# Perceiver layer on one core: the first feed-forward product by seven combined block products instead of eight plain ones, in three of its four blocks

## The reference

```
x = x + xattn(layernorm(x), ctx)
x = x + attn(layernorm(x))
x = x + ffn(layernorm(x))
ffn: h   = relu(x @ w1.T + b1)              # hidden width H = 2048
     out = q16(q8(h) @ q8(w2).T + q16(b2))  # q8: 4 exponent, 3 mantissa bits
```

## Time and profile before

| | |
|---|---|
| median of 3 runs | 946.39 us (945.07 to 947.18) |
| the profiled execution | 946.05 us, of which the span is 944.2 us |
| PE busy over the span | 926.6 us (98%) |
| DVE, ACT, POOL busy | 542.0, 583.9, 494.0 us |
| granted TensorE clock | 1.00 |

### The profile page before, as it was taken

One profiled execution on the slowest core, in us unless ns is written; L12 is line 12 of the kernel. 1 busy time (PEld: TensorE's weight loads), 2 busy tenths in 40 slices (PEclk: granted clock), 3 DMA queues, 4 the chain that ended last, 5 costly groups with the idle time before them and its releaser, 6 DMA issues.

```text
span 944.2 us, 19392 instructions
## 1 busy us (share of the span) xinstructions
PE 926.6 (98%) x7405; PEld 576.6 (61%) x7408; DVE 542.0 (57%) x980; ACT 583.9 (62%) x1095; POOL 494.0 (52%) x379
## 2 busy tenths in 40 slices
PE   6999999999999999999999999999999999999998
PEld 3556666666666666666666666666665545544443
DVE  7455655556555565555655556556677725375533
ACT  4477777777777777777777777777677122222220
POOL 2356666565566666656556666886777451110000
PEclk9999999999999999999999999999999999999999
DMA  8257576876866776677666678869875321213212
GB/s 300 68 159 141 130 131 139 163 146 130 140 135 132 137 142 128 136 155 158 132 127 145 135 135 163 185 121 182 157 141 108 90 56 40 59 33 107 88 34 78
DMA packets 313211, 120.05 MB, mean 127 GB/s; under 512 B 289952, under 2 KB 289952, under 8 KB 313120
## 3 DMA queue, kind: packets, MB, share of 16 engines
q1 hardware_dynamic: 298128, 89.97, 50.8%
q10 hardware_dynamic: 14992, 28.84, 9.5%
HBM read 45.36 MB, written 2.10 MB: 50 GB/s over the span
## 4 chain that ended last, share of the span: by engine, by line
PE 96%; ACT 2%; DMA 1%; POOL 0%; issue 0%; DVE 0%; SPq 0%; ACTq 0%; POOLq 0%
PE v_ps L422 27%; PE k_ps L422 26%; PE e_ps L422 17%; PE e_ps L463 9%; PE o_ps L485 6%; PE o_ps L488 3%; PE o_ps L650 3%; PE v_ps L615 1%; DMA wq_raw<-in_xwq 1%; PE o_ps L624 1%; DMA raw<-in_ctx_t 1%; ACT xt_h L728 0%; PE o_ps L515 0%; PE o_ps L512 0%; PE o_ps L509 0%; POOL ctx_l L1261 0%
## 5 line engine op out<-in xcount | busy, mean ns | idle before, releaser
L1269 POOL TENSOR_TENSOR p_l<-p_f,p_h 128x1024 f16<-128x1024 f32 x128 | 272.6, 2130 | 228.9 <-ACT p_f L792 228.8
L790 ACT ACTIVATE p_h<-e_ps,bias 128x512 f16<-128x512 f32 x256 | 175.9, 687 | 5.1 <-POOL p_l L1269 2.4
L792 ACT ACTIVATE p_f<-e_ps,bias 128x512 f32<-128x512 f32 x256 | 176.7, 690 | 0.0
L991 DVE TENSOR_TENSOR k_l<-k_ps,k_h 128x512 f16<-128x512 f32 x128 | 88.6, 692 | 145.6 <-ACT k_h L764 145.6
L983 DVE TENSOR_TENSOR v<-v_ps,v 128x512 f16<-128x512 f32 x128 | 88.9, 694 | 122.3 <-ACT v L756 122.3
L996 DVE TENSOR_REDUCE q_max<-e_ps 128x2 f32<-128x1024 f32 x128 | 150.8, 1220 | 8.2 <-PE e_ps L463 0.2
L422 PE MATMUL v_ps<-wv_h,ctx_h 128*128 128x256 f16 x768 | 126.3, 273 | 1.5 <-DVE v L983 1.5
L422 PE MATMUL v_ps<-wv_h,ctx_l 128*128 128x256 f16 x768 | 125.7, 273 | 0.0
L422 PE MATMUL v_ps<-wv_l,ctx_h 128*128 128x256 f16 x768 | 125.7, 273 | 0.0
L1261 POOL TENSOR_TENSOR ctx_l<-raw,ctx_h 128x1536 f16<-128x1536 f32 x32 | 100.2, 3130 | 22.1 <-ACT ctx_h L745 21.5
L485 PE MATMUL o_ps<-v,pt_h 128*128 128x130 f16 x1024 | 106.0, 220 | 0.6 <-issue 0.6
(11 more groups left out here) (169 smaller groups left out, 1249.3 us busy)
## 6 DMA issues: line engine op xcount, KB each, us to landing
raw<-in_ctx_t ACTq DMA_DIRECT2D x26, 768.0 KB, 5.3
w_raw<-in_w_t SPq DMA_DIRECT2D x32, 256.0 KB, 2.8
raw<-in_ctx_t SPq DMA_DIRECT2D x6, 768.0 KB, 4.9
pt_h<-p_h SPq DMA_TRANSPOSE x128, 3.3
pt_l<-p_l SPq DMA_TRANSPOSE x128, 3.2
out<-xr SPq DMA_DIRECT2D x8, 256.0 KB, 2.0
x_in<-in_x ACTq DMA_DIRECT2D x6, 256.0 KB, 9.2
o_all<-in_x ACTq DMA_DIRECT2D x6, 256.0 KB, 4.4
```

The lines of the kernel that those rows point to most:

```text
L790: act.activation(p_h[:, s % H_RING, h, :], e_ps[s % 2][:, h, :], ACT.Exp, scale=EXP_SCALE, bias=bias[:, n % 2, h, q:q + 1]).then_inc(p_hi, 1)
L792: act.activation(p_f[:, s % F_RING, h, :], e_ps[s % 2][:, h, :], ACT.Exp, scale=EXP_SCALE, bias=bias[:, n % 2, h, q:q + 1]).then_inc(p_ful ...
L991: dve.tensor_tensor(k_l[:, n % 2, cols], k_ps[:, :], k_h[:, n % 2, cols], ALU.subtract).then_inc(k_split, 1)
L1269: pool.tensor_tensor(p_l[:, s % L_RING, :, :], p_f[:, s % F_RING, :, :], p_h[:, s % H_RING, :, :], ALU.subtract).then_inc(p_split, 1)
```

## The change

Block 0 stays. In blocks 1 to 3 the 4 hidden tiles by 8 token rows are seen as 2 by 2 blocks of weights (W11, W12, W21, W22; hidden side by input side) and 2 by 2 blocks of tokens. Winograd's form of Strassen's scheme makes the four results from seven products instead of eight. Each product is of 2 hidden tiles (the halves p = 0, 1) by 512 tokens over 256 inputs, so one half is 3 passes by 2 chunks = 6 matmuls (`combined_product`). The tokens are combined once, the weights once per block, and the results are added up in between:

- **POOL** combines the layer-normed tokens in `o_all` in place (`combine_tokens`, 3 subtractions for each of 4 pairs of rows), and for each block scales W11, W12 and W22 to their high halves and makes four sums S1 to S4 of weight blocks. It also makes the low halves of four of the token pieces.
- **ACT** rounds tokens and sums to high halves, copies products 1, 5 and 6 out of PSUM to float32 (`keep_x`, `keep_p5`), rounds `w2` to 8 bits (`w2_high`), which DVE did before, and rounds the 8 results of a block (`part_round`).
- **DVE** makes the low halves of all seven weight pieces (`weights_low`), adds up three of the four results of each half (`add_up`), widens `w2` and spreads the rounded results.
- **SP** turns the combined token halves by 16 more DMA transposes, and loads block 2's `w1` tiles once all seven pieces of block 1 are split.
- The combined products use all eight PSUM banks (blocks 1 and 3 four of them, block 2 the other four), and the second layer moves to `t_bank`.

The core of the diff:

```
+        products = [(1, 1, 0), (1, 2, 0)]
+        for block_at in range(1, BLOCKS):
+            last = block_at == BLOCKS - 1
+            products += [(block_at, i, p) for i, p in ((1, 1), (2, 1), (5, 0), (6, 0), (5, 1), (3, 0), (6, 1), (3, 1), (7, 0))]
+            products += [] if last else [(block_at + 1, 1, 0)]
+            products += [(block_at, 7, 1)]
+            products += [] if last else [(block_at + 1, 2, 0)]
+            products += [(block_at, 4, 0), (block_at, 4, 1)]
...
-            for block in range(1, BLOCKS):
-                for j in range(8):
-                    hidden_product(block, j)
+            for b, i, p in products:
+                combined_product(b, i, p)
...
+            def combined_product(b, i, p):
+                pe.wait_ge(ws_split, weight_at(b, WEIGHT_OF[i]) + 1)
...
+                elif i == 5:
+                    pe.wait_ge(c_ready, added_at(b, "C11", p) + 1)
+                elif i == 6:
+                    pe.wait_ge(x_kept, kept_at(b, 1, p) + 1)
+                elif i == 3:
+                    pe.wait_ge(p5_kept, 2 * (b - 1) + p + 1)
+                elif i == 7:
+                    pe.wait_ge(x_kept, kept_at(b, 6, p) + 1)
+                elif i == 4:
+                    pe.wait_ge(c_ready, added_at(b, "C22", p) + 1)
...
+                for n, (wi, xi) in enumerate(((0, 0), (1, 0), (0, 1))):
+                    for c in range(2):
+                        mm = pe.matmul(acc[:, :], w[wi][:, c, :], x[xi][c], start=(first and n == 0 and c == 0),
+                                       stop=(n == 2 and c == 1), skip_group_check=True)
```

The lists of the other engines. POOL, after its last instruction of before:

```
+            for k in range(4):
+                combine_tokens(k)
+            weights_high(1, "W11")
+            weights_high(1, "W12")
+            combine_weights(1)
+            for k in range(4):
+                tokens_low(k)
+            weights_high(1, "W22")
+            for b in range(2, BLOCKS):
+                weights_high(b, "W11")
+                weights_high(b, "W12")
+                combine_weights(b)
+                weights_high(b, "W22")
```

ACT in a block (`more`: not the last), with the weights of the next:

```
+                keep_x(b, 1, 1)
+                part_round(b, "C11", 1)
+                keep_p5(b, 0)
+                w2_high(5 * b - 5)
+                keep_x(b, 6, 0)
+                keep_p5(b, 1)
+                w2_high(5 * b - 4)
+                part_round(b, "C12", 0)
+                keep_x(b, 6, 1)
+                w2_high(5 * b - 3)
+                part_round(b, "C12", 1)
+                w2_high(5 * b - 2)
+                if more:
+                    weights_high(b + 1, "S1")
+                part_round(b, "C22", 0)
+                w2_high(5 * b - 1)
+                if more:
+                    keep_x(b + 1, 1, 0)
+                    weights_high(b + 1, "S2")
...
+                part_round(b, "C22", 1)
```

DVE: the tail of block 0, then the beginning of a block:

```
+            def first_hidden_block():
                 for j in range(8):
+                    spread(j, j % 4, j // 4)
...
+                    if 2 <= j < 6:
+                        tokens_low(j - 2)
+                    elif j >= 6:
+                        weights_low(1, WEIGHTS[j - 6])
+                for name in WEIGHTS[2:]:
+                    weights_low(1, name)
+                    if name == "S2":
+                        add_up(1, "C11", 0)
+            def hidden_block(b):
+                more = b < BLOCKS - 1
+                if b > 1:
+                    weights_low(b, "W22")
+                add_up(b, "C11", 1)
...
+                part_spread(b, "C11", 1)
+                w2_round(5 * b - 5)
+                w2_round(5 * b - 4)
+                if more:
+                    weights_low(b + 1, "W11")
+                add_up(b, "C12", 0)
+                w2_round(5 * b - 3)
+                if more:
+                    weights_low(b + 1, "W12")
+                add_up(b, "C12", 1)
+                part_spread(b, "C12", 0)
+                w2_round(5 * b - 2)
+                if more:
+                    weights_low(b + 1, "S1")
+                add_up(b, "C22", 0)
```

with `WEIGHTS = ["W11", "W12", "S1", "S2", "S4", "S3", "W22"]`. `add_up` reads one operand from PSUM and one from SBUF; `weights_low` and `tokens_low` read both from SBUF. SP's list after the turned tokens:

```
-                if i >= 4:
+                if i >= 8:
+                    sp.wait_ge(ws_split, len(WEIGHTS) * (i // 4 - 1))
+                elif i >= 4:
                     sp.wait_ge(w1_split, i - 3)
...
+            for j in range(8, 12):
+                load_w1(j)
+            for i in range(2, 7):
+                load_w2(i)
+            for j in range(12, 16):
+                load_w1(j)
```

More of the change, by code:

```diff
@@ L40 @@
 BLOCKS = HC // 4
+C_RING = 3
 def place(nc, base, spec):
@@ new lines, in perceiver_kernel @@
+        SUMS = ["S1", "S2", "S4", "S3"]
+        PLAIN = ["W11", "W12", "W22"]
+        TOKENS_AT = {6: 0, 5: 2, 7: 4, 4: 6}
+        products = [(1, 1, 0), (1, 2, 0)]
+        parts = [(1, "C11", 0)]
+        for block_at in range(1, BLOCKS):
[5 more added lines that the diff above has]
+            products += [(block_at, 4, 0), (block_at, 4, 1)]
+            parts += [(block_at, c, p) for c, p in (("C11", 1), ("C12", 0), ("C12", 1), ("C22", 0), ("C22", 1))]
+            parts += [] if last else [(block_at + 1, "C11", 0)]
+            parts += [(block_at, "C21", 0), (block_at, "C21", 1)]
@@ new lines, in perceiver_kernel, with product_at, part_at, kept_at @@
+        added = [part for part in parts if part[1] != "C21"]
+        kept = [product for product in products if product[1] in (1, 6)]
+        def product_at(*product):
+            return products.index(product)
+        def part_at(*part):
+            return 8 + parts.index(part)
+        def kept_at(*product):
+            return kept.index(product)
+        def added_at(*part):
+            return added.index(part)
+        def weight_at(b, name):
+            return len(WEIGHTS) * (b - 1) + WEIGHTS.index(name)
@@ new lines, in spread, with part_spread, add_up @@
+            def spread(m, row, half):
+                dve.wait_ge(h_q8, m + 1)
+                dve.tensor_copy(hq[:, row, 4 * half:4 * half + 4, :],
+                                h_8[:, m % 2, :].rearrange("p (r n) -> p r n", r=4)).then_inc(h_ready, 1)
+            def part_spread(b, c, p):
+                spread(part_at(b, c, p), 4 * b + 2 * p + (c[1] == "2"), c[2] == "1")
+            def add_up(b, c, p):
+                i = added_at(b, c, p)
+                dve.wait_ge(prod_filled, product_at(b, {"C11": 2, "C12": 3, "C22": 7}[c], p) + 1)
+                if c == "C22":
+                    dve.wait_ge(p5_kept, 2 * (b - 1) + p + 1)
+                    bank, other = sum_bank(b, p), p5[:, p, :]
+                else:
+                    dve.wait_ge(x_kept, kept_at(b, {"C11": 1, "C12": 6}[c], p) + 1)
+                    bank, other = second_bank(b, p), x_f[:, p, :]
+                if i >= C_RING:
+                    dve.wait_ge(h_q8, part_at(*added[i - C_RING]) + 1)
+                else:
+                    dve.wait_ge(read_filled, B)
+                dve.tensor_tensor(c_f[:, i % C_RING, :], bank[:, :], other, ALU.add).then_inc(c_ready, 1)
@@ L1220, in _ @@
             norm(B + 7)
-            for block in range(BLOCKS):
-                hidden_block(block, block < BLOCKS - 1)
+            first_hidden_block()
+            for b in range(1, BLOCKS):
+                hidden_block(b)
             dve.wait_ge(b2_ready, 1)
```

325 lines of the change are left out of this document (264 added, 61 removed).

## The result

The changed kernel took 970.07 us (968.77 to 971.81, 5 runs) against 946.34 (944.83 to 947.18, 5 runs) beside it: 1.0255 times as long, 95% interval 1.0242 to 1.0268. That is 23.7 us more; 965.1 had been predicted, 951 to 973 as the range.

What follows compares the result with a forecast made beforehand. PE was taken as the bound, then made to wait for ACT, DVE and POOL: waits of 7.4 + 7.3 + 7.5 + 4.3 = 26.5 us less 7.8 removed, +18.7 on the median 946.4, gives 965.1 us; range 951 to 973.

Steps and rivals of the forecast that it cites:

- Bound and removal: Blocks 1 to 3: PE was the bound; 36 matmuls fewer save 7.8 us; the stage grows from 62 to about 81.
- The upper end, 971: Whole kernel: some 971 us if held DVE instructions and POOL's strided pieces cost a fifth more, 5 to 6 us.
- Start of block 1: Up to product (5, 1), which waits for W22, scaled last by POOL and ready at 864.1: 7.4 us late.
- Rest of block 1: From product (5, 1): late w1 loads and ACT-DVE hand-overs delay (4, 0) by 5.0 and (4, 1) by 2.3: 7.3 us.
- `x + 3.7`: Block 1: when the fourth w1 load for block 2 lands, counted from x, the start of product (5, 1).
- Blocks 2 and 3: Block 2 repeats block 1's waits, 7.5 us late; block 3 has no weights to prepare, 4.3 us late.
- The port: Beside busy POOL, DVE's casts and low halves wait for POOL's next boundary, about 1.3 us each; without it 958.6, not 965.1.
- Rival (a): Waits, but no holding of DVE at the port shared with POOL: +12.2, 958.6 us; chance 0.20.
- Rival (c): PE also runs slower after its stalls, up to five stretches, half absorbed: +5, 970 us; chance 0.15.
- Rival (b): PE stays the bound after the first wait: 944.0 us, or 939 with W22 early too; chance 0.10.

Runs made afterwards that it cites:

- the reordered kernel: Changed kernel with early w1 loads in a second buffer, ACT's high halves ahead of rounds, block 0's low halves first, W22 scaled earlier: 950.67 us, 1.0048.
- the two-block kernel: Seven products only in blocks 2 and 3, the four reorderings, DMA queue relieved, DVE's last sums and first weight splits earlier; against the kernel before: 944.23 us, 0.9986.
- the first three: Each alone on the changed kernel: early w1 loads with second buffer, 964.84 us; ACT's high halves ahead of rounds, 962.26; block 0's low halves before a cast, 968.74.

## Why the prediction was right, and where it was off

**Bound and removal.** As predicted, PE stops being the bound: 36 matmuls fewer, and 83.3 us for the stage (81 foreseen). Its busy time did not fall by 7 to 8 us, though: half pace filled most of that up.

**The size.** The loss is 23.7 us for 18.7, and 25.8 in the profiled execution: 7 more than the sum has. That 970 is inside the range is owed in part to luck. The upper end, 971, was worked out for POOL's pieces and holds that cost more than taken, and they did, for about 3 us; the longer loads behind most of the other 4 were in no term of it.

**Start of block 1.** 5.9 us for 7.4, but from a block 0 that ended 4.7 us late: product (5, 1) started 10.6 us after it was due. The mechanism was as told, W11 and W12 behind DVE's held instructions and then W22 behind POOL's whole list; the three waits are 1.40, 1.61 and 2.36 us. What was mis-sized is that list: POOL had W22 ready at 867.22, where 864.1 was reckoned. It began 0.4 us later, and each of its kinds of work took a little longer (the four token pairs 15.2 us with their gaps for 13.6, W22 1.93 for 1.5). That is the whole of the 3.1 us by which (5, 1) started after the forecast's 865.55.

**Rest of block 1.** 11.4 for 7.3, the largest miss. The four loads took up to 6.0 us to land where 2.7 was taken from a median, so POOL started W11 3.1 us after `x + 3.7`. PE also lost 1.5 us at half pace before the C22 sums and 1.2 in product (4, 1). Early loads gave back 5.2 us and with them PE kept full pace here (clock 1.00 from 875 to 890 us); moving `w2` gave back 7.8. The hand-over chain was thus sized well and the loads too short.

**Blocks 2 and 3.** 7.4 and 4.2 for 7.5 and 4.3, and the C22 waits at their places.

**Block 0.** The step that failed was one that the text did not take: it reckoned POOL's work from 834 us as a delay for block 1 only. But the port that it argued from holds DVE's casts in block 0 as well, in front of the rows that PE turns there. This cost block 0 4.7 us in the profile. They do not come on top of POOL's list, which ran on meanwhile and set the start of (5, 1): moving the cast gave back 1.3 us at most by the medians. A wait also stood where no sign of the prediction had one.

**The port.** Held casts and low halves are shown: 1251 and 1410 ns beside a busy POOL, and in the changed kernel 543 and 1247, all in the mean. Rival (a), waits without holding, is out as a mechanism. How many of the 23.7 us are the port's stays open: 2.8 at most in blocks 2 and 3 of the reordered kernel, and the 6.5 us that the forecast gave it (965.1 less 958.6) were not isolated.

**Rival (c), pace.** Half of it came true: the clock fell in three stretches, and 970 us is its number, closer than the forecast's. But with the clock kept up in two of them the time stayed within what can be told apart, so pace does not explain the difference of 5 us by itself, and that its number fits is chance. It was set aside for a row with a wait of 0.99 us; here waits of 2.0 to 2.9 us did it.

**Rival (b), PE stays the bound.** Wrong for this order of the lists. It asked that the work in front of the C12 sum be early and the turns behind it overlapped, with 944.0 or 939. With those orders mended the three-block kernel came to 950.7, still 6.7 us above the first and 12 above the second. The 944.2 of the two-block kernel is another sum, with 24 matmuls fewer instead of 36, so that it meets 944.0 is chance. Of the 23.7 us lost, 19.4 were the order of the lists and the one buffer for the loads; whether a better order would also bring in the 7.8 us of the removed matmuls, no run shows.

## What to carry to other kernels

When work leaves the bounding engine and every product begins to hang on others, a sum of busy times says little: write out the list of each engine, and the DMA queue's, and look for the last release at each gate. One early piece before a late gate is worth little; four together gave 19.4 us where the first three, each by itself, add up to 14.3. Price work on GpSimd also by what it does to VectorE wherever it runs, the stage before the changed one included. Take the time of a load from loads issued together, if they are issued together. And try the restructured part where its preparation has a full block of plain work to hide in: that was the only place here where it did not lose.

## What was not expected of the hardware

- 50 GpSimd additions that nobody needs cost 14.9 us. Beside them VectorE's SBUF casts, 0.43 us long, last 1.25.
- The granted clock fell to half after PE's waits of 2.43, 2.87 and 1.98 us and stayed there for 3 to 5 us. After those of 2.34 and 2.15 us at 913.67 and 917.27 it did not fall, nor after one of 2.76 us at 869.05 in the kernel with early loads, nor after one of 0.99 us. After every longer wait from 836 us on in the traces (3.40 in the kernel before beside the additions, 4.68, 4.76 and 6.58 in the others) half pace followed. What tells the shorter ones apart stays open. Matmuls into an unread bank in the gaps kept it at 1.00, but the time came out the same.
- Four loads of 256 KB, issued in a row, took 7.6 us (6.0 in block 2) from the first issue to the start of GpSimd's first instruction on them, and up to 6.0 us each to land, where the earlier trace rows had a median of 2.7.
- A DMA transpose holds SP's queue for 1.2 to 1.3 us. With 16 of them in its list, loads written behind them went out late, and waits of 6.6 and 4.8 us on PE came of it.
